# Relation stage of a graph network: messages in three bf16 parts beside constant matmuls, and two relations in one matmul

## What is computed

```
h1  = relu(einsum('ni,rij->nrj', x, weight1) + bias1)
h2  = einsum('nrj,rjo->nro', h1, weight2)
msg = h2[src, rel_type] * norm
agg = segment_sum(msg, dst, num_segments=N)
x   = layernorm(x + relu(agg + bias2))
```

## Time and profile before

| | us |
|---|---|
| median of three runs | 10305.17 |
| the profiled execution | 10305.41 |
| its span, first to last instruction | 10303.6 |
| relation_nodes | 8877.5 to 9070.2 |
| relation_pass | 9070.2 to 10279 |
| finish | 10279 to 10303 |

### The profile page before, as it was taken

One profiled execution on the slowest core, in us unless ns is written; L12 is line 12 of the kernel. 1 busy time (PEld: TensorE's weight loads), 2 busy tenths in 40 slices (PEclk: granted clock), 3 DMA queues, 4 the chain that ended last, 5 costly groups with the idle time before them and its releaser, 6 DMA issues. The chain is left out here.

```text
span 10303.6 us, 320385 instructions
## 1 busy us (share of the span) xinstructions
PE 7532.6 (73%) x107650; PEld 6085.0 (59%) x107651; DVE 5955.4 (58%) x19882; ACT 3749.0 (36%) x13000; POOL 4698.3 (46%) x6243
## 2 busy tenths in 40 slices
PE   2999995676657849976994997699588789832332
PEld 1777764555547749966993896699334344433332
DVE  6444448888866778987997899699510000011111
ACT  3222215777753326753772675477200000100000
POOL 0677770000006635532551553255365677256665
PEclk9999998888879979987996998799699899755555
DMA  8222224555429949955992996599488999311112
GB/s 322 58 59 60 59 54 146 181 181 185 142 85 306 310 144 256 264 164 152 262 263 61 257 262 172 148 263 264 135 320 324 343 366 365 129 34 18 18 18 18
DMA packets 1832085, 1846.79 MB, mean 179 GB/s; under 512 B 1450037, under 2 KB 1467989, under 8 KB 1786741
## 3 DMA queue, kind: packets, MB, share of 16 engines
q1 hardware_dynamic: 1717890, 1668.62, 52.6%
q0 software_dynamic: 112016, 153.10, 5.9%
q10 hardware_dynamic: 2016, 22.94, 0.6%
HBM read 1481.79 MB, written 360.62 MB: 179 GB/s over the span
## 5 line engine op out<-in xcount | busy, mean ns | idle before, releaser
L1616 POOL TENSOR_TENSOR s_rest<-s_msg 128x196 f32<-128x196 f32 x1488 | 764.9, 514 | 1906.5 <-ACT s_msg L1598 1810.0
L1208 PE MATMUL s_gotd<-m_table_d,s_hot 128*128 x17856 | 1363.4, 205 | 204.1 <-DMA s_hot<-OHT 195.0
L1598 ACT ACTIVATE s_msg<-s_gotd,s_es 128x49 f32<-128x49 f32 x5952 | 1310.4, 304 | 48.4
L1208 PE MATMUL s_gotq<-m_table_s,s_hot 128*128 x17856 | 1279.9, 185 | 8.5 <-issue 8.5
L1208 PEld LDWEIGHTS s_gotd<-m_table_d,s_hot 128*128 128x128 bf16 x17856 | 989.4, 96 | 293.9 <-DMA s_hot<-OHT 196.2
L1878 POOL DMA_INDIRECT REC<-m_sums x800 | 957.0, 1196 | 354.1 <-issue 346.2
L456 POOL DMA_INDIRECT REC<-rec,place x800 | 943.3, 1179 | 329.3 <-issue 214.9
L2141 POOL DMA_INDIRECT l_row<-H,l_rec x816 | 789.6, 968 | 614.4 <-DMA l_rec<-REC 335.0
L1649 DVE TENSOR_REDUCE s_tops<-s_mt 128x512 f32 (+1 forms) x1488 | 1013.7, 681 | 4.5 <-PE s_mt L1559 4.3
L1911 PE MATMUL p_acc<-p_row,p_feats 128*64 128x512 f32 (+1 forms) x4032 | 898.6, 569 | 158.4 <-DMA p_row<-ADJ 156.0
L1208 PEld LDWEIGHTS s_gotq<-m_table_s,s_hot 128*128 128x128 bf16 x17856 | 992.3, 97 | 5.4 <-issue 5.3
(11 more groups left out here) (418 smaller groups left out, 18945.9 us busy)
## 6 DMA issues: line engine op xcount, KB each, us to landing
s_hot<-OHT SPq DMA_DIRECT2D x1488, 384.0 KB
p_row<-ADJ SPq DMA_DIRECT2D x288, 1600.0 KB
s_rec<-REC SPq DMA_DIRECT2D x1488, 98.0 KB
OHT<-a_turned SPq DMA_DIRECT2D x372, 384.0 KB
g_hot<-OHT SPq DMA_DIRECT2D x372, 384.0 KB
ADJ<-a_acc POOLq DMA_DIRECT2D x25, 3200.0 KB
REC<-fill SPq DMA_DIRECT2D x124, 624.0 KB, 10.3
g_rec<-REC SPq DMA_DIRECT2D x372, 108.0 KB
```

The costliest lines, as they stand in the source:

```text
L1208: last = nc.tensor.matmul(out, hot, table[k][:, bass.ds(at, w)], start=(k == 0), stop=(k == 2))
L1598: last = nc.scalar.activation(msg[:, b % KEPT, j], gotd[b % KEPT][:, j, SW:2 * SW], ACT.Copy, scale=es[:, b % 2, j:j + 1])
L1616: nc.gpsimd.tensor_tensor(rest[:, b % KEPT].rearrange("p g w -> p (g w)"), msg[:, b % KEPT].rearrange("p g w -> p (g w)"), upper(msg[:, b ...
```

## The change

In relation_nodes two relations go through one matmul. Hidden multiplies by the weight1 of two relations side by side and gives 96 rows. Weight2 becomes a block-diagonal 96x96 matrix for each pair: POOL zeroes it (s_zero), and SP loads the two diagonals after that; the bias is loaded twice. The 25 blocks give 96 columns each, five blocks in one of six PSUM banks, which DVE copies in one operation, 20 in all. H2 is written in four DMAs, each behind its pair of relations, in runs of 384 bytes.

The diff, without the loads and waits that the words above tell:

```diff
-        h1T = room.sb("h1T", [H, 2, NB * P])
+        h1T = room.sb("h1T", [PAIR, 2, NB * P])
-        w2 = room.sb("w2", [H, RELS, H])
+        w2 = room.sb("w2", [PAIR, TWOS, PAIR])
-        h2p = [room.ps(f"h2p{b}", [P, 3, 512]) for b in range(2)]
+        h2p = [room.ps(f"h2p{b}", [P, FIVE, PAIR]) for b in range(BANKS)]
...
-                        nc.tensor.matmul(banks[m % 2][0:H, 0:n], w1[:, r], xT[:, 4 * q * P:4 * q * P + n],
-                                         start=True, stop=True).then_inc(s_h1, 1)
+                        nc.tensor.matmul(banks[m % 2][0:PAIR, 0:n],
+                                         w1[:, 2 * t:2 * t + 2].rearrange("i r j -> i (r j)"),
+                                         xT[:, 4 * q * P:4 * q * P + n], start=True, stop=True).then_inc(s_h1, 1)
...
+                        for i in range(FIVE):
+                            node = c * FIVE + i
+                            last = nc.tensor.matmul(h2p[k % BANKS][:, i], h1T[:, t % 2, node * P:(node + 1) * P],
+                                                    w2[:, t], start=True, stop=True)
+                        last.then_inc(s_h2, 1)
...
-        oh = room.sb("oh", [P, SLOTS, G, P])
+        oh = room.sb("oh", [P, SLOTS, G, P], BF16)
+        rest = room.sb("rest", [P, SLOTS, G, SW])
+        least = room.sb("least", [P, SLOTS, G, SW], BF16)
+        turning = room.ps("turning", [P, 512])
+        plain = room.sb("plain", [P, 512], BF16)
...
+        def upper(ap):
+            return ap.bitcast(BF16).rearrange("p (w h) -> p w h", h=2)[:, :, 1]
...
                     for j in range(G):
-                        last = add_sums(nc, sums, at[j], oh[:, b, j], msg[:, b, j])
-                    last.then_inc(s_agg, 1)
+                        for third in (upper(msg[:, b, j]), upper(rest[:, b, j]), least[:, b, j]):
+                            last = add_sums(nc, sums, at[j], oh[:, b, j], third)
+                        if j == G - 1:
+                            last.then_inc(s_agg, 1)
+                        for _ in range(3):
+                            nc.tensor.matmul(turning[:], mem["ident_bf"][:], plain[:], start=True, stop=True)
...
+                    whole = msg[:, b].rearrange("p g w -> p (g w)")
+                    after = rest[:, b].rearrange("p g w -> p (g w)")
+                    ch.step(v.tensor_tensor(after, whole, upper(whole), ALU.subtract))
+                    ch.step(v.tensor_tensor(least[:, b].rearrange("p g w -> p (g w)"), after, upper(after),
+                                            ALU.subtract))
                     dve.sem_inc(s_msg, 1)
```

More of the change, by code:

```diff
@@ L2032, in relation_nodes @@
 def relation_nodes(nc, mem, io):
+    PAIR, FIVE = 2 * H, 5
+    TWOS, PARTS, BANKS = RELS // 2, NB // FIVE, 6
     with ExitStack() as ctx:
@@ L2036, in relation_nodes @@
         xT = room.sb("xT", [H, NB * P])
-        h1T = room.sb("h1T", [H, 2, NB * P])
+        h1T = room.sb("h1T", [PAIR, 2, NB * P])
         h2 = room.sb("h2", [P, NB, RELS * H])
         w1 = room.sb("w1", [H, RELS, H])
-        w2 = room.sb("w2", [H, RELS, H])
-        b1 = room.sb("b1", [H, 1])
-        s_w, s_turned, s_copied, s_h1, s_h1c, s_h2, s_h2c, s_out = (
-            room.sem(n) for n in ("s_w", "s_turned", "s_copied", "s_h1", "s_h1c", "s_h2", "s_h2c", "s_out"))
+        w2 = room.sb("w2", [PAIR, TWOS, PAIR])
+        b1 = room.sb("b1", [PAIR, 1])
+        s_zero, s_w, s_turned, s_copied, s_h1, s_h1c, s_h2, s_h2c, s_out = (
+            room.sem(n) for n in ("s_zero", "s_w", "s_turned", "s_copied", "s_h1", "s_h1c", "s_h2", "s_h2c", "s_out"))
         banks = [room.ps(f"bank{b}", [P, 512]) for b in range(2)]
-        h2p = [room.ps(f"h2p{b}", [P, 3, 512]) for b in range(2)]
+        h2p = [room.ps(f"h2p{b}", [P, FIVE, PAIR]) for b in range(BANKS)]
         with nc.Block() as block:
@@ L2049, in _ @@
                 sp.dma_start(w1[:], io["L3_gnn_weight1"].rearrange("r i j -> i r j")).then_inc(s_w, 16)
[L2050 to L2054, removed]
+                for k in range(2):
+                    sp.dma_start(b1[k * H:(k + 1) * H], io["L3_gnn_bias1"].rearrange("(p o) -> p o", o=1)
+                                 ).then_inc(s_w, 16)
+                sp.wait_ge(s_zero, 1)
+                for k in range(2):
+                    sp.dma_start(w2[k * H:(k + 1) * H, :, k * H:(k + 1) * H],
+                                 io["L3_gnn_weight2"].rearrange("(t k) i j -> k i t j", k=2)[k]).then_inc(s_w, 16)
+                for t in range(TWOS):
+                    sp.wait_ge(s_h2c, (t + 1) * PARTS)
+                    sp.dma_start(mem["H2"].rearrange("(c p) w -> p c w", p=P)[:, :, t * PAIR:(t + 1) * PAIR],
+                                 h2[:, :, t * PAIR:(t + 1) * PAIR]).then_inc(s_out, 16)
+                sp.wait_ge(s_out, 16 * TWOS)
+            @block.gpsimd
+            def _(pool):
+                nc.gpsimd.memset(w2[:], 0.0).then_inc(s_zero, 1)
             @block.scalar
@@ L2058, in _ @@
                 copy_turned(nc, act, xT, H, banks, s_turned, s_copied)
[L2059 to L2062, removed]
+                act.wait_ge(s_w, 80)
+                for t in range(TWOS):
+                    if t >= 2:
+                        act.wait_ge(s_h2, (t - 1) * PARTS)
                     for q in range(QUADS):
                         n = min(4, NB - 4 * q) * P
-                        m = r * QUADS + q
+                        m = t * QUADS + q
                         act.wait_ge(s_h1, m + 1)
-                        nc.scalar.activation(h1T[:, r % 2, 4 * q * P:4 * q * P + n], banks[m % 2][0:H, 0:n],
+                        nc.scalar.activation(h1T[:, t % 2, 4 * q * P:4 * q * P + n], banks[m % 2][0:PAIR, 0:n],
                                              ACT.Relu, bias=b1[:, 0:1]).then_inc(s_h1c, 1)
@@ L2073, in _, with hidden @@
                 pe.wait_ge(s_copied, QUADS)
-                pe.wait_ge(s_w, 48)
-                def hidden(r):
+                pe.wait_ge(s_w, 80)
+                def hidden(t):
                     for q in range(QUADS):
                         n = min(4, NB - 4 * q) * P
-                        m = r * QUADS + q
+                        m = t * QUADS + q
                         if m >= 2:
                             pe.wait_ge(s_h1c, m - 1)
-                        nc.tensor.matmul(banks[m % 2][0:H, 0:n], w1[:, r], xT[:, 4 * q * P:4 * q * P + n],
-                                         start=True, stop=True).then_inc(s_h1, 1)
+                        nc.tensor.matmul(banks[m % 2][0:PAIR, 0:n],
+                                         w1[:, 2 * t:2 * t + 2].rearrange("i r j -> i (r j)"),
+                                         xT[:, 4 * q * P:4 * q * P + n], start=True, stop=True).then_inc(s_h1, 1)
@@ L2085, in _ @@
                 hidden(0)
[L2086 to L2095, removed]
+                for t in range(TWOS):
+                    if t + 1 < TWOS:
+                        hidden(t + 1)
+                    pe.wait_ge(s_h1c, (t + 1) * QUADS)
+                    for c in range(PARTS):
+                        k = t * PARTS + c
+                        if k >= BANKS:
+                            pe.wait_ge(s_h2c, k - BANKS + 1)
+                        for i in range(FIVE):
[3 more added lines that the diff above has]
+                        last.then_inc(s_h2, 1)
@@ L2097, in _ @@
             @block.vector
             def _(dve):
[L2099 to L2105, removed]
+                for t in range(TWOS):
+                    for c in range(PARTS):
+                        k = t * PARTS + c
+                        dve.wait_ge(s_h2, k + 1)
+                        nc.vector.tensor_copy(h2[:, c * FIVE:(c + 1) * FIVE, t * PAIR:(t + 1) * PAIR],
+                                              h2p[k % BANKS][:]).then_inc(s_h2c, 1)
@@ L2120, in relation_pass @@
         sums = room.ps("sums", [P, 3, 512])
+        turning = room.ps("turning", [P, 512])
+        plain = room.sb("plain", [P, 512], BF16)
+        s_plain = room.sem("s_plain")
         table = mem["H2"].rearrange("n (r w) -> (n r) w", w=H)
+        def upper(ap):
+            return ap.bitcast(BF16).rearrange("p (w h) -> p w h", h=2)[:, :, 1]
         with nc.Block() as block:
@@ L2134, in _ @@
             def _(pool):
+                nc.gpsimd.memset(plain[:], 1.0).then_inc(s_plain, 1)
                 def rows(n, b, lap):
@@ L2154, in add @@
                     for j in range(G):
[L2155 to L2156 removed]
+                        for third in (upper(msg[:, b, j]), upper(rest[:, b, j]), least[:, b, j]):
[4 more added lines that the diff above has]
+                            nc.tensor.matmul(turning[:], mem["ident_bf"][:], plain[:], start=True, stop=True)
+                pe.wait_ge(s_plain, 1)
                 zero_sums(nc, mem, sums)
@@ L2167, in messages @@
                 def messages(n, b, lap):
-                    ch = Chain(dve, s_dve, n * 2)
+                    ch = Chain(dve, s_dve, n * 4)
```

(2 more changed lines are left out.)

## The result

The changed kernel took 10381.27 us, the median of four runs (10373.17 to 10389.45), beside 10304.92 for the kernel before on the same chip. The ratio is 1.0074 [1.0063, 1.0086]: **slower, by some 76 us**, 0.7%. The forecast was slower by 230. The profiled execution took 10383.90 (span 10382.1).

The account below looks back on a forecast made before the run. PE bounds relation_nodes; in the relation pass PE alternates between full pace and a crawl that makes POOL wait. 10305 - 95 (nodes) + 322 (pass) = 10532, said as 10535 us; wide range 10035 to 10780, own range 10330 to 10790.

Parts of the forecast that it names:

- Nodes, -95: In relation_nodes: half the hidden and h2 matmuls and a shorter H2 transfer save 95 us (54 to 140).
- the low end: In relation_nodes: an h2 pass with 96 columns still takes 0.216 us; the high end was 0.376.
- DVE's two operations: In the relation pass: two more DVE operations a group, 1.75 us instead of 1.05, covered below POOL's 5.0.
- the crawl: In the relation pass: slow PE stretches, records 0.70 us or a multiple apart, alternating with full pace; expected to stay.
- the rival that forecast 10063: In the relation pass: constants raise the clock and end the crawl, POOL sets the pace, -147 us there; chance 0.32.
- The size, +322: Relation pass: 7.5 us a group, 1530 us in all, 322 more than before, from pricing cycles of full pace and crawl.
- q: PE's time for one relation-pass group at full pace: 2.9 to 5.7 us, taken near 3.6.
- the 9 us: In each relation-pass cycle: after POOL fills the slots, 9 us pass until PE is quick and POOL back.
- The line for q 2.9: Cheapest relation-pass cycle: 5.8 groups ended, 51 us for 7.8 groups, 6.5 us each, 1330 in all.
- Records price the crawl: Main case, relation pass: PE's 48 records instead of 16 make a crawling group 46 to 60 us, not 20; chance 0.53.
- PE as the bound, 10240: Rival, relation pass: crawl ends but clock stays 1.2 GHz, 5.7 to 6.4 us a group; 10165 to 10308; chance 0.09.
- Only the nodes count, 10210: Rival: the slow stretches in the relation pass stay and cost nothing more, only relation_nodes gains; chance 0.06.

Follow-up runs that it names:

- nodes only: The change's new relation_nodes with the relation_pass of the kernel before; 10213.41 us, ratio 0.9902 to the kernel before.
- few and long: Against nodes only: two fp32 constant matmuls of 512 columns added behind each group's fp32 sums; 10276.63 us, ratio 0.9964 to the kernel before.
- short constants: Against the changed kernel: constant matmuls of 32 columns instead of 512, same number of records; 10298.27 us, ratio 0.9982 to the kernel before.
- 160 columns: Against nodes only: a POOL memset of 160 bf16 columns behind each gather; 10190.49 us, ratio 0.9896 to the kernel before.
- the longer step: Against the changed kernel: a POOL memset of 160 columns behind each gather; 10331.16 us, ratio 1.0024 to the kernel before.

## Why the prediction was right in direction and wrong in size

- **Nodes, -95: right** (-93; nodes only took 101 us off, by its ratio). An h2 pass stayed at 0.213 us, the low end. The last transfer took 7.9 instead of 6, within its bounds.
- **DVE's two operations: hidden**, as far as the runs tell; none took them out alone. The 20 to 40 us for gathers beside DVE were not seen: 967 ns a gather against 968. The 0.7 us at the very end is a small part of what came there: the drain grew by 20 us, since PE, and not DVE, was behind.
- **That the crawl stays, and does not go with the clock: right.** 44 records in 47 us are 1.07 us each, where the text had 1.26; that makes 51 us for a group of 48, within the 46 to 60 of the text (20 us and 32 more steps of 0.70 are 42, not 46). The crawl began at full clock, and few and long raised the clock without ending it; so the rival that forecast 10063 falls. The Trainium skill, "TensorE: Matmul & The Clock Gate", Part 1, "HAM oscillation", ties throttling to a PE that waits between its pieces; the trace agrees so far that the clock falls behind the crawl and rises in the bursts.
- **The size, +322: this step failed, the price of a cycle, and in it POOL's pause.** The time lies within the range, but the change is a third of the forecast. The sum gives a cycle q, 14 us, 5 us for each group to fill, and 9 us. POOL issues in all of it but q and the 9, so with q 3.6 it stands 12.6 us in a cycle of some 5.3 groups, 7.4 us a group (the text has 7.5). But the 9 us were read off POOL's waiting, and q is in them already: in the earlier trace rows PE is quick at 9624.02, and POOL is back 3.6 us later, at the end of its 10.05. A pause of the kernel after:

```profile
9283.52 0.94 POOL L2168 DMA_INDIRECT l_row<-H,l_rec  x1 [0.30 <-issue]
...
9287.13 1.44 PE L2187 MATMUL l_turning<-l_plain,m_ident_bf 128*128 128x512 bf16 x3 [0.51 <-issue]
...
9291.57 0.95 POOL L2168 DMA_INDIRECT l_row<-H,l_rec  x1 [7.10 <-DVEq L2214]
```

PE is quick 3.6 us behind POOL's last issue, where it took 7.4, and POOL is back 4.4 us after that. The 43 pauses last 7.0 us beyond the step on average, some 300 us in all, where the sum has 204 / 5.3 x 12.6 = 485. With the 9 us counted once, the prediction's own numbers give 6.7 us a group and some 1370, +160, beside the measured +167.5. That this comes so near is partly luck: both the pause (7.0) and the groups of a cycle (4.6) are smaller than in the sum, and the two errors cancel.
- **q was right.** The timeline shows 5.6 us a group at first and 2.9 later; over the bursts of the trace, PE is at full pace for 13 us on average and ends 3.7 groups, 3.5 us each, where I took 3.6. But full pace lasts only 8.6 us after POOL's return, not 14.
- **The range was drawn wrong as well.** The line for q 2.9 fills five groups, though 5.8 ended less 2.75 brought leave three; filled as in the other two lines it is some 6.9 us a group, 1410 in the pass, above the measured 1376.5. And 1815 in the pass is 10816, not 10790.
- **"Records price the crawl" is half the truth.** By records alone, short constants would have cost what the change cost; they cost 81 of its 168 us. PE's time counts as well: with as many records, long constants cost 88 us more. A reason that fits is that full pace lasts only some 13 us, and what PE cannot end in it is left to the crawl. Both were in the sum (14/q, and one group in the crawl), but the text named only the records.
- **PE as the bound, 10240: wrong.** PE is busy 849 of 1376 us, and POOL keeps its step between pauses. **Only the nodes count, 10210: wrong**, that is where the kernel without the pass's change stands.
- **Where my picture of the pass fell.** I took all of POOL's waiting before, 158 us, as the price of PE's crawl. With fulfilled waits on POOL PE never crawled, and the pass was 15 us shorter, no more. The runs with the pass of before lie between 1185 and 1229 whatever is done to buffers, bytes or PE's pace, and even a quarter of the sums left 1151. Some 1.41 us a gather (1150.9 / 816) is the least that any run here shows over a whole pass, against a step of 1.25 that POOL keeps for a stretch.

**What stays open.** What it is that gives PE, or POOL's sequencer, one instruction per 0.70 us while gathers come 1.25 us apart, and for a while after. It is not the bytes, not the number of buffers, not the clock; whether it goes with the number of rows gathered was not tried. A backlog would fit: at 1.41 us of work a gather and 1.25 of step, 184 gathers leave 184 x 0.16 = 29 us and 40 leave 6.4, beside the 31.5 and 7.4 us that PE took to get back to full pace; but that is worked out afterwards. The rate is doubtful: at a step of 1.365 it would leave 10 us after 216 gathers, and with 160 columns PE took 3.3. The Trainium skill, "NOTIFIC — the notification-queue block", section 7.1, has a rule that would fit too: a full queue of trace records can be set to stall the engine that writes them. No run here shows that unit, and all the profiles here come from executions that were recorded, so whether the crawl is there in one that is not was not tried. Of the 128 us that stay with the longer step no run told the parts apart.

## What to carry to other kernels

An engine that is idle for two thirds of a stage can still be what everybody waits for: look at the spacing of its records, and whether that changes when another engine pauses, before calling its idle time free. Where one producer issues faster than the whole can take, the time comes back as pauses; a slightly longer step cost nothing here (94 us of steps for 118 of pauses) and gave back 50 us where PE had much to do. When a sum is built from measured stretches, ask of each whether another term is in it already: here PE's first group stood inside POOL's pause and was charged twice. Work that was added to keep TensorE's clock up did not pay in this stage: the clock went from 0.50 to 0.71 in the pass, and the pass from 1209 to 1376 us.

## What the runs showed that I had not expected

- Six waits that are already fulfilled, 43 ns each at the median, moved the 0.70 us steps from PE to POOL's sequencer: "remote" of DVE fell from 605.5 us to 4.2, and the time from 10213 to 10198.
- More buffers made the pass no shorter: it took 1214.9 with 12 and 1229.4 with 17, and 1208.0 with 6; and PE crawled on for 31.5 us after a run of 184 gathers, while DMA moved 2 to 4 GB/s.
- An fp32 pass on 128 columns of weights cost 0.213 us with 96 columns and 0.216 with 48, at half clock.
